# Causal mask of attention scores: added by VectorE in PSUM instead of by a third TensorE product, with two PSUM copies moved from VectorE to ScalarE

## The chip, the cores and the metric

One core of a Trainium2 chip runs the whole program. The metric is the device time of one execution in microseconds (us). The engines of the core are TensorE (PE in the rows, with its weight loads as PEld), VectorE (DVE), ScalarE (ACT), GpSimd (POOL) and SyncE (SP), which here only issues DMAs.

## The reference

The program computes a layer of causal attention plus a quantised linear layer, and after it a second layer of another kind. The change lies in the causal attention. Per batch entry (8 of them, 512 rows, 16 heads of 64):

```python
scores = jnp.einsum('bnqd,bnkd->bnqk', q, k) / jnp.sqrt(jnp.float32(L))
causal = jnp.arange(s)[None, :] <= jnp.arange(s)[:, None]
scores = jnp.where(causal, scores, -1000000000.0)
attn = jax.nn.softmax(scores, axis=-1)
attended = jnp.einsum('bnqk,bnkd->bnqd', attn, v)
```

## The kernel before, in words

The program has three stages: loading and scaling (about the first 140 us), a long software pipeline of "rings" that does the attention and the quantised layer, and the second layer. A ring `n` belongs to one pair of heads; there are 8 pairs in each of 8 batch entries, so 64 rings that matter, and a few to fill. With `b, r = n // 8, n % 8`, every engine walks through its own written-out order of steps, `ring(n)`, and the engines meet at semaphores. Nothing is reordered: an instruction that waits holds back all that stand behind it on its engine.

In ring `n` these things happen together:

- The scores of the next pair, `n + 1`, for head `h` = 0 and then 1. A head has four row blocks (tiles 0 to 3) of 128, 256, 384 and 512 columns, since the columns above the diagonal block are left out. Tile 3 lies in PSUM bank `sx`, tiles 0 and 2 together in `sy`, tile 1 in `sz`. TensorE makes each with two f16 products (L1328, L1329) and a third (L1330) that adds the mask to the diagonal block, as the product of an identity and a bf16 mask.
- VectorE takes the row maxima (`maxima`, L1021), ScalarE the exponentials with their row sums (`exps`, L698), VectorE the reciprocals of the sums (`inverse`, L1029), GpSimd scales the rows (`normalise`, L529).
- The rows of pair `n` are transposed by TensorE (`pt(n, j, h)`, L1341, column block `j`, 4 - `j` transposes) into one bank for head 0 (`pt0`) and one for head 1 (`pt1`). Each bank is copied out (`pt_whole(n, j)`): head 0 by ScalarE (L706), head 1 by VectorE (L1036). `pt(n, j, h)` waits for the copy of `j - 1`, as each head has but one bank. `av(n)` (L1355) then multiplies with the values; ScalarE's L714 follows it, once in each ring.
- The queries and keys of a later pair: `evens(n + 5)` and `odds(n + 5)` on TensorE, `even_terms` (L1000, L1001) and `odd_terms` (L1011, L1012) on VectorE, `rotate` (L501, L503) on GpSimd, `high_e` (L673) and `high_o` (L681) on ScalarE, then DMAs to and from a scratch. Rings 59 to 63 have none of this.
- From the second batch entry on, the output projection of the entry before (`attended`, L1370): 6 products after the scores (0,2) of head 0 and 6 after the scores (1) of head 1; in rings with `r % 4 == 0` the first of these is `ffn` (4 products) and the second has 12.

The orders of TensorE and ScalarE in a ring decide most of what follows. TensorE: `scores(n+1,0,(1))`, `v(n)`, `pt(n,0,0)`, `scores(n+1,0,(0,2))`, attended or ffn, `pt(n,0,1)`, `scores(n+1,0,(3,))`, `pt(n,1,0)`, `pt(n,1,1)`, `evens`, `scores(n+1,1,(1,))`, attended, `pt(n,2,0)`, `pt(n,2,1)`, `scores(n+1,1,(0,2))`, `pt(n,3,0)`, `scores(n+1,1,(3,))`, `pt(n,3,1)`, `odds`, `av(n)`. GpSimd: `normalise(n,1)`, `rotate`, two low parts, `normalise(n+1,0)`.

Of the kernel before, what the change touches and what calls it, by code (L numbers as in the profile page):

```python
# [10 lines left out]
P = 128  # L11
NT = SQ // P
# [9 lines left out]
MASKED = -1e30  # L22
OFF = [P * i * (i + 1) // 2 for i in range(NT + 1)]
TOFF = [sum(P * (NT - a) for a in range(j)) for j in range(NT + 1)]
# [19 lines left out]
def build(nc, x_d, weights_d, w8_d, bqk_d, vec_d, thr_d, gate_d, tab_d, out_d):  # L44
    f32, f16, bf16 = mybir.dt.float32, mybir.dt.float16, mybir.dt.bfloat16
    i8, i32, u32 = mybir.dt.int8, mybir.dt.int32, mybir.dt.uint32
    ALU = mybir.AluOpType
    ACT = mybir.ActivationFunctionType
# [7 lines left out]
    with ctx:  # L56
        def sb(name, shape, dt):
            return ctx.enter_context(nc.sbuf_tensor(name, shape, dt))

        def sem(name):  # L60
            return ctx.enter_context(nc.semaphore(name))
# [5 lines left out]
        wl = sb("wl", [P, C_END], f16)  # L67
        w8 = sb("w8", [P, KT, D], bf16)
        ident = sb("ident", [P, P], f32)
        identb = sb("identb", [P, P], bf16)  # L70
        maskb = sb("maskb", [P, P], bf16)

        bcol = sb("bcol", [P, NQ, 2, 2], f32)
        cosq = sb("cosq", [P, SQ], f32)
# [64 lines left out]
        kz = [carve(4 * SQ, f16).rearrange("p (h s) -> p h s", h=4) for _ in range(2)]  # L139
        vf = carve(NT * P).rearrange("p (t c) -> p t c", t=NT)  # L140
        pr = [carve(OFF[NT]) for _ in range(4)]
        ptf = [carve(TOFF[NT]) for _ in range(2)]
# [48 lines left out]
        consts = sem("consts")  # L191
# [39 lines left out]
        v_mm = sem("v_mm")  # L231
        vf_done = sem("vf_done")
        s_done = sem("s_done")
        max_done = sem("max_done")
        exp_done = sem("exp_done")
        rc_done = sem("rc_done")
        norm_done = sem("norm_done")
        pt_done = [sem(f"pt_done{h}") for h in range(2)]
        ptf_done = [sem(f"ptf_done{h}") for h in range(2)]
# [52 lines left out]
        def no_phase(f):  # L292

            return not 0 <= f < NPH

        def absent(n):

            return not 0 <= n < NR

        def after(engine, s, count):  # L300

            if not isinstance(count, int) or count > 0:
                engine.wait_ge(s, count)
# [41 lines left out]
        pj, wo, sx, sy, sz, pt0, pt1, ob = banks  # L345

        S_ORDER = [1, 0, 2, 3]
        s_tile = {3: sx[:, 0:512], 0: sy[:, 0:128], 2: sy[:, 128:512], 1: sz[:, 0:256]}

        S_BANK = {1: 1, 0: 2, 2: 2, 3: 3}  # L350
# [112 lines left out]
        def _(pool):  # L463

            pool.memset(ident[:], 0.0).then_inc(consts, 1)
            pool.memset(identb[:], 0.0).then_inc(consts, 1)
            pool.memset(maskb[:], 0.0).then_inc(consts, 1)
            pool.wait_ge(consts, 3)
            for m in (ident, identb):
                pool.affine_select(out=m[:], in_=m[:], compare_op=ALU.not_equal, fill=1.0, base=0,  # L470
                                   pattern=[[-1, P]], channel_multiplier=1).then_inc(consts, 1)
            pool.affine_select(out=maskb[:], in_=maskb[:], compare_op=ALU.is_ge, fill=MASKED, base=0,
                               pattern=[[-1, P]], channel_multiplier=1).then_inc(consts, 1)

            pool.wait_ge(wmax_done, NG)
# [2 lines left out]
            for g in range(NG):  # L478
                pool.wait_ge(whi_done, g + 1)
                if g in (G_Q, G_K):  # L480
                    for src, (high, low) in halves(g):
                        last = pool.tensor_tensor(low, src, high, ALU.subtract)
# [146 lines left out]
        @block.scalar  # L629
        def _(act):  # L630

            act.wait_ge(consts, 6)
            act.activation(nm3[:, 0, 0:1], ident[:, 0:1], ACT.Exp)
            def xt_high(batches):

# [26 lines left out]
            for t in range(2):  # L662
                act.activation(fbow[:, t], banks[7][:, 0:D], ACT.Copy)
                last = act.activation(wsxw[:, t], banks[7][:, D:2 * D], ACT.Copy)
# [10 lines left out]
            def high_o(f):  # L675

                if no_phase(f):
                    return
                act.wait_ge(r1_done, f + 1)
                after(act, hio_sent, 16 * f)  # L680
                act.activation(hi_o, r_o, ACT.Copy).then_inc(hio_done, 1)  # L681
# [8 lines left out]
            def exps(n, h, par, tiles):  # L690

                if absent(n):
                    return
                slot = 2 * par + h
                for i in tiles:

                    act.wait_ge(max_done, 4 * (2 * n + h) + {1: 1, 0: 3, 2: 3, 3: 4}[i])
                    act.activation(pr[slot][:, OFF[i]:OFF[i + 1]], s_tile[i], ACT.Exp, bias=nm[:, slot, i:i + 1],  # L698
                                   accum_out=sm[:, slot, i:i + 1]).then_inc(exp_done, 1)

            def pt_whole(n, j):

                if absent(n):
                    return
                act.wait_ge(pt_done[0], 4 * n + j + 1)
                act.activation(ptf[0][:, TOFF[j]:TOFF[j + 1]], pt0[:, 0:P * (NT - j)], ACT.Copy).then_inc(ptf_done[0], 1)  # L706

            def out_high(n):

# [6 lines left out]
            def ring(n):  # L716

                e, o = (n + 1) % 2, n % 2
                out_high(n - 1)
                exps(n + 1, 0, e, (1,))  # L720
                v_whole(n)
                pt_whole(n, 0)
                high_e(n + AHEAD - 1)
                exps(n + 1, 0, e, (0, 2))
                high_o(n + AHEAD - 1)
                pt_whole(n, 1)
                exps(n + 1, 0, e, (3,))
                pt_whole(n, 2)
                exps(n + 1, 1, e, (1, 0, 2))
                pt_whole(n, 3)  # L730
                exps(n + 1, 1, e, (3,))
# [130 lines left out]
        def _(dve):  # L862
# [97 lines left out]
            for g, by, dsts in ((G_Q, L ** -0.5, (cosq, sinq)), (G_K, 1.0, (cosk, sink))):  # L960
                for a, dst in enumerate(dsts):
                    dve.tensor_scalar(dst[:], tabraw[:, a], sc[:, g:g + 1], by, ALU.mult, ALU.mult)
                last = dve.tensor_scalar(bcol[:, :, g - G_Q], bcol[:, :, g - G_Q], inv[:, g:g + 1], None, ALU.mult)
# [4 lines left out]
            for k in range(KT):  # L968
                dve.tensor_scalar(diag[:, k], ident[:], fbo[:, k:k + 1], None, ALU.mult)
                last = dve.tensor_scalar(diag[:, KT + k], ident[:], vec[:, V_FS + k:V_FS + k + 1], None, ALU.mult)  # L970
# [43 lines left out]
            def maxima(n, h, par, tiles):  # L1014

                if absent(n):
                    return
                slot = 2 * par + h
                for i in tiles:
                    dve.wait_ge(s_done, 3 * (2 * n + h) + S_BANK[i])  # L1020
                    dve.tensor_reduce(nm[:, slot, i:i + 1], s_tile[i], AX.X, ALU.max, negate=True).then_inc(max_done, 1)  # L1021

            def inverse(n, h, par):
# [7 lines left out]
            def pt_whole(n, j):  # L1031

                if absent(n):
                    return
                dve.wait_ge(pt_done[1], 4 * n + j + 1)
                dve.tensor_copy(ptf[1][:, TOFF[j]:TOFF[j + 1]], pt1[:, 0:P * (NT - j)]).then_inc(ptf_done[1], 1)  # L1036
# [38 lines left out]
            def row_statistics(b):  # L1075

                dve.wait_ge(x1_done, 2 * b + 2)
                statistics(b * NT, b + NB)

            def ring(n):  # L1080

                b, r, e = n // NP, n % NP, (n + 1) % 2
                tail = b >= 1
                maxima(n + 1, 0, e, (1,))
                out_low(n - 1)
                maxima(n + 1, 0, e, (0, 2))
                pt_whole(n, 0)
                if tail and r % 4 == 0:
                    ffn_part(b - 1, r // 4)
                maxima(n + 1, 0, e, (3,))  # L1090
                pt_whole(n, 1)
                even_terms(n + AHEAD)
                inverse(n + 1, 0, e)
                maxima(n + 1, 1, e, (1,))
                pt_whole(n, 2)
                maxima(n + 1, 1, e, (0, 2, 3))
                pt_whole(n, 3)
                odd_terms(n + AHEAD)
                inverse(n + 1, 1, e)
                if n >= 0 and r >= NP - 4:  # L1100
                    quantise(b, r - NP + 4)
                if tail and r % 4 == 3:
                    residual(b - 1, r // 4)
                if b >= 2 and r == 1:
                    row_statistics(b - 2)
# [145 lines left out]

        @block.tensor
        def _(pe):
            pe.wait_ge(consts, 6)
            for b in range(NB):
                u = b % 2
                pe.wait_ge(xn1_done, b + 1)
# [1 line left out]
                for k in range(KT):  # L1259
                    for c in range(NT):  # L1260
                        last = pe.transpose(banks[2 * u + k][:, c * P:(c + 1) * P], xn1[u][:, c, k * P:(k + 1) * P], ident[:])
# [54 lines left out]
            def scores(n, h, tiles):  # L1316

                if absent(n):
                    return
                g = 2 * n + h  # L1320
                par, hh = n // 2 % 2, n % 2 * 2 + h
                if h == 0 and tiles[0] == 1 and hh == 0:
                    pe.wait_ge(q_in[par], 64 * (n // 4 + 1))
                    pe.wait_ge(k_in[par], 96 * (n // 4 + 1))
                after(pe, exp_done, 4 * g - 4 + {1: 1, 0: 3, 3: 4}[tiles[0]])
                for i in tiles:
                    out, q = s_tile[i], qs[par][:, hh, i * P:(i + 1) * P]
                    pe.matmul(out, q, kd[par][:, hh, 0:(i + 1) * P], start=True, stop=False)  # L1328
                    pe.matmul(out, q, kz[par][:, hh, 0:(i + 1) * P], start=False, stop=False)  # L1329
                    last = pe.matmul(out[:, i * P:(i + 1) * P], identb[:], maskb[:], start=False, stop=True)  # L1330
                last.then_inc(s_done, 1)

            def pt(n, j, h, par):
# [81 lines left out]
            for a in range(2 * KT):  # L1415
                last = pe.matmul(banks[7][:, a * P:(a + 1) * P], ones, diag[:, a], start=True, stop=True)
# [202 lines left out]
```

## Time and profile before

| | |
|---|---|
| median of 3 runs | 1176.16 us (1173.99 to 1178.44) |
| profiled execution, its own time | 1175.19 us |
| its span, first to last instruction | 1173.40 us |
| granted TensorE clock, mean share of full speed | 0.982 |
| TensorE products busy | 1023.0 us, 87% of the span |
| VectorE busy | 892.0 us, 76% |
| GpSimd busy | 767.5 us, 65% |
| ScalarE busy | 691.4 us, 59% |

The profile is one execution. A busy time counts an instruction from its start to its end, and neighbours on one engine overlap: a 128-column product is recorded with 0.22 us but the next one starts 0.06 us later. So what a product costs is read from the starts, not from its duration. An idle time stands in brackets with the instruction that ended it.

### The profile page before, as it was taken

To read this page: it belongs to the slowest core of one execution; us is meant where nothing else is said; L and a number is where in the kernel's file an instruction comes from. 1 tells how busy PE (TensorE), PEld (TensorE's weight loads), DVE (VectorE), ACT (ScalarE), POOL (GpSimd) and SP (SyncE) were. 2 spreads that over 40 slices of the span, in tenths; PEclk is the share of its full clock that TensorE was granted. 3 is DMA by queue.
4 is the path that set the end of the run, shared out by engine and by line. 5 is a ranking of instruction groups with operands and counts; after the bars stand their busy time and mean duration, and the time that the engine had idled before them with its cause. 6 is when DMAs were issued, how large, how long until landed. Compare 5 with 4: busy or idle time off the path is not lost.

```text
span 1173.4 us, 23304 instructions
## 1 busy us (share of the span) xinstructions
PE 1023.0 (87%) x7944; PEld 665.5 (57%) x7944; DVE 892.0 (76%) x1869; ACT 691.4 (59%) x1831; POOL 767.5 (65%) x949
## 2 busy tenths in 40 slices
PE   2004599999999999999999999999999965899988
PEld 1002266666666766766666676676667742454444
DVE  7695577776777777777777777777777637999996
ACT  1252366766666666666666666666667604766764
POOL 0081677777877777786777777687776515756762
PEclk9998999999999999999999999999999986999999
DMA  9203433342233233223323322322332000010001
GB/s 347 83 0 126 144 102 97 96 131 82 87 112 100 82 105 121 82 95 109 95 87 110 112 85 96 109 91 89 105 97 82 1 1 1 1 37 19 19 28 45
DMA packets 99700, 100.11 MB, mean 85 GB/s; under 512 B 12928, under 2 KB 94848, under 8 KB 99200
## 3 DMA queue, kind: packets, MB, share of 16 engines
q1 hardware_dynamic: 99584, 98.63, 25.8%
q8 instruction: 65, 1.06, 0.4%
q14 instruction: 51, 0.42, 0.1%
HBM read 56.64 MB, written 41.94 MB: 84 GB/s over the span
## 4 chain that ended last, share of the span: by engine, by line
PE 73%; DVE 18%; issue 3%; DMA 2%; ACT 2%; SPq 1%; POOL 1%; DVEq 0%; ACTq 0%; POOLq 0%
PE bank L1267 24%; PE bank L1355 13%; PE bank L1341 12%; PE bank L1370 7%; PE bank L1328 6%; PE bank L1329 5%; DVE arena L1179 3%; PE bank L1330 2%; DMA x_sb<-in_x 2%; PE bank L1517 2%; DVE nm L1149 1%; DVE arena L916 1%; DVE wmax L950 1%; DVE arena L1198 1%; DVE nm L1021 1%
## 5 line engine op out<-in xcount | busy, mean ns | idle before, releaser
L529 POOL TENSOR_SCALAR arena<-arena,rc 128x128 f32<-128x128 f32 (+3 forms) x512 | 276.0, 559 | 197.2 <-DVE rc L1029 197.2
L698 ACT ACTIVATE arena<-bank,nm 128x256 f32<-128x256 f32 (+3 forms) x512 | 268.4, 527 | 83.9 <-DVE nm L1021 73.7
L1021 DVE TENSOR_REDUCE nm<-bank 128x1 f32<-128x256 f32 (+3 forms) x512 | 229.9, 480 | 108.5 <-PE bank L1330 105.0
L1341 PE MATMUL bank<-ident,arena 128*128 128x128 f32 x1280 | 216.6, 277 | 4.8 <-DVE arena L1036 4.4
L1341 PEld LDWEIGHTS bank<-ident,arena 128*128 128x128 f32 x1280 | 143.7, 141 | 41.2 <-DVE arena L1036 20.3
L706 ACT ACTIVATE arena<-bank 128x512 f32<-128x512 f32 (+3 forms) x256 | 111.3, 435 | 79.6 <-PE bank L1341 79.4
L1329 PE MATMUL bank<-arena 128*128 128x256 f16 (+3 forms) x512 | 153.4, 300 | 0.0
L1355 PE MATMUL bank<-arena 128*64 128x512 f32 (+3 forms) x1024 | 152.0, 439 | 0.0
L1328 PE MATMUL bank<-arena 128*128 128x256 f16 (+3 forms) x512 | 147.4, 301 | 2.7 <-ACT arena L698 2.7
L1036 DVE COPY arena<-bank 128x512 f32<-128x512 f32 (+3 forms) x256 | 124.1, 485 | 23.8 <-PE bank L1341 20.0
L1355 PEld LDWEIGHTS bank<-arena 128*64 128x64 f32 x1024 | 67.8, 136 | 94.3 <-issue 71.3
L1267 PE MATMUL bank<-xsh,wh 128*128 128x512 f16 x256 | 98.1, 383 | 17.7 <-DVE arena L1001 9.6
L1330 PE MATMUL bank<-maskb,identb 128*128 128x128 bf16 x512 | 112.2, 219 | 0.0
L1370 PE MATMUL bank<-wh,arena 128*128 128x256 f16 x512 | 103.2, 278 | 7.2 <-DVE arena L1065 7.2
L698 ACT ACTIVATION_READ_ACCUMULATOR arena<-bank,nm 128x1 f32 x512 | 102.6, 200 | 0.0
L714 ACT ACTIVATE arena<-bank,bvs 128x512 f16<-128x512 f32 x64 | 44.0, 687 | 96.4 <-PE bank L1355 96.4
L1267 PE MATMUL bank<-xsl,wh 128*128 128x512 f16 x256 | 98.0, 383 | 0.0
L1267 PE MATMUL bank<-xsh,wl 128*128 128x512 f16 x256 | 98.0, 383 | 0.0
L501 POOL TENSOR_TENSOR arena<-arena 128x512 f32<-128x512 f32 x64 | 81.4, 1273 | 18.6 <-DVE arena L1012 18.6
L1267 PE MATMUL bank<-wh,xsh 128*128 128x128 f16 x512 | 89.1, 219 | 1.1 <-DVE arena L1012 1.1
L1267 PE MATMUL bank<-wh,xsl 128*128 128x128 f16 x512 | 89.1, 219 | 0.0
L1267 PE MATMUL bank<-wl,xsh 128*128 128x128 f16 x512 | 89.1, 219 | 0.0
(148 smaller groups left out, 2225.7 us busy)
## 6 DMA issues: line engine op xcount, KB each, us to landing
arena<-scr SPq DMA_DIRECT2D x320, 128.0 KB, 2.5
scr<-arena SPq DMA_DIRECT2D x256, 128.0 KB, 1.7
x_sb<-in_x SPq DMA_DIRECT2D x8, 512.0 KB, 6.5
arena<-in_weights SPq DMA_DIRECT2D x2, 2048.0 KB, 12.4
out<-x_sb SPq DMA_DIRECT2D x16, 256.0 KB, 2.2
xscr<-xsh SPq DMA_DIRECT2D x8, 256.0 KB, 2.3
xscr<-xsl SPq DMA_DIRECT2D x8, 256.0 KB, 2.2
xsh<-xscr SPq DMA_DIRECT2D x8, 256.0 KB, 3.1
```

What stands on the lines that cost most here:

```text
L529: last = pool.tensor_scalar(pr[slot][:, OFF[i]:OFF[i + 1]], pr[slot][:, OFF[i]:OFF[i + 1]], rc[:, slot, i:i + 1], 1.0, ALU.mult, ALU.mult)
L698: act.activation(pr[slot][:, OFF[i]:OFF[i + 1]], s_tile[i], ACT.Exp, bias=nm[:, slot, i:i + 1], accum_out=sm[:, slot, i:i + 1]).then_inc(e ...
L706: act.activation(ptf[0][:, TOFF[j]:TOFF[j + 1]], pt0[:, 0:P * (NT - j)], ACT.Copy).then_inc(ptf_done[0], 1)
L1021: dve.tensor_reduce(nm[:, slot, i:i + 1], s_tile[i], AX.X, ALU.max, negate=True).then_inc(max_done, 1)
L1036: dve.tensor_copy(ptf[1][:, TOFF[j]:TOFF[j + 1]], pt1[:, 0:P * (NT - j)]).then_inc(ptf_done[1], 1)
L1267: last = pe.matmul(out, lhs, rhs, start=(a == 0), stop=(a == len(pairs) - 1))
L1328: pe.matmul(out, q, kd[par][:, hh, 0:(i + 1) * P], start=True, stop=False)
L1329: pe.matmul(out, q, kz[par][:, hh, 0:(i + 1) * P], start=False, stop=False)
L1330: last = pe.matmul(out[:, i * P:(i + 1) * P], identb[:], maskb[:], start=False, stop=True)
L1341: last = pe.transpose(banks[5 + h][:, (i - j) * P:(i - j + 1) * P], pr[2 * par + h][:, OFF[i] + j * P:OFF[i] + (j + 1) * P], ident[:])
L1355: last = pe.matmul(ob[h * L:(h + 1) * L, j * P:SQ], vf[:, j, h * L:(h + 1) * L], ptf[h][:, TOFF[j]:TOFF[j + 1]], start=(j == 0), stop=(j = ...
L1370: last = pe.matmul(bank[:, t * D:(t + 1) * D], o[:, slot, rows], w[:, p, :], start=(p == 0 and a == 0 and t == 0), stop=(p == NP - 1 and a ...
```

## The change

TensorE's third product goes. VectorE adds an f32 mask to the diagonal block in PSUM before it takes the maxima: one add for tile 1, one for tiles 0 and 2 together (their diagonal blocks are columns 0 to 127 and 384 to 511 of `sy`), one for tile 3. After each add it waits for its own semaphore `masked`. Of head 1's four copies `j` = 0 and `j` = 2 go from VectorE to ScalarE. The score semaphore is counted per bank as before. On GpSimd the making of two bf16 constants is replaced by that of one f32 constant.

```diff
@@ scalar, ring
                 pt_whole(n, 0)
                 high_e(n + AHEAD - 1)
                 exps(n + 1, 0, e, (0, 2))
+                pt_whole(n, 0, 1)
                 high_o(n + AHEAD - 1)
                 pt_whole(n, 1)
                 exps(n + 1, 0, e, (3,))
                 pt_whole(n, 2)
+                pt_whole(n, 2, 1)
                 exps(n + 1, 1, e, (1, 0, 2))
                 pt_whole(n, 3)
@@ vector, maxima
                 slot = 2 * par + h
+                dve.wait_ge(s_done, 3 * (2 * n + h) + S_BANK[tiles[0]])
+                if tiles == (0, 2):
+                    both = sy[:].rearrange("p (a c) -> p a c", c=P)[:, 0:NT:NT - 1]
+                    dve.tensor_tensor(both, both, maskf[:].unsqueeze(1).broadcast_to([P, 2, P]), ALU.add).then_inc(masked, 1)
+                else:
+                    diagonal = s_tile[tiles[0]][:, tiles[0] * P:]
+                    dve.tensor_tensor(diagonal, diagonal, maskf[:], ALU.add).then_inc(masked, 1)
+                dve.wait_ge(masked, 3 * (2 * n + h) + S_BANK[tiles[0]])
                 for i in tiles:
-                    dve.wait_ge(s_done, 3 * (2 * n + h) + S_BANK[i])
                     dve.tensor_reduce(nm[:, slot, i:i + 1], s_tile[i], AX.X, ALU.max, negate=True).then_inc(max_done, 1)
@@ vector, ring
                 maxima(n + 1, 0, e, (0, 2))
-                pt_whole(n, 0)
                 if tail and r % 4 == 0:
                     ffn_part(b - 1, r // 4)
                 maxima(n + 1, 0, e, (3,))
@@
                 maxima(n + 1, 1, e, (1,))
-                pt_whole(n, 2)
-                maxima(n + 1, 1, e, (0, 2, 3))
+                maxima(n + 1, 1, e, (0, 2))
+                maxima(n + 1, 1, e, (3,))
                 pt_whole(n, 3)
@@ tensor, scores
                     pe.matmul(out, q, kd[par][:, hh, 0:(i + 1) * P], start=True, stop=False)
-                    pe.matmul(out, q, kz[par][:, hh, 0:(i + 1) * P], start=False, stop=False)
-                    last = pe.matmul(out[:, i * P:(i + 1) * P], identb[:], maskb[:], start=False, stop=True)
+                    last = pe.matmul(out, q, kz[par][:, hh, 0:(i + 1) * P], start=False, stop=True)
```

## Rows read from the trace of the kernel before

**Rows 1.** Busy time by stretch: us, busy (x count) per engine, PEclk, DMA share, GB/s

```profile
400.00:600.00 200.00, 200.00 (x1716) 137.00 (x1714) 152.28 (x332) 128.48 (x375) 151.01 (x198) 1.00 0.31 99
```

**Rows 2.** Timeline, ScalarE, the instruction after each `av`: start us, duration us

```profile
191.20 0.69 ACT L714 ACTIVATE arena<-bank,bvs 128x512 f16<-128x512 f32 x1 [1.48 <-PE bank L1355]
203.35 0.69 ACT L714 ACTIVATE arena<-bank,bvs 128x512 f16<-128x512 f32 x1 [1.48 <-PE bank L1355]
...
495.21 0.69 ACT L714 ACTIVATE arena<-bank,bvs 128x512 f16<-128x512 f32 x1 [1.55 <-PE bank L1355]
508.30 0.69 ACT L714 ACTIVATE arena<-bank,bvs 128x512 f16<-128x512 f32 x1 [1.68 <-PE bank L1355]
520.96 0.69 ACT L714 ACTIVATE arena<-bank,bvs 128x512 f16<-128x512 f32 x1 [1.55 <-PE bank L1355]
```

**Rows 3.** Chain that ended last, one ring: start us, us, what

```profile
523.57 0.06 PE bank L1330
...
525.21 0.84 PE bank L1341 x6
526.05 1.29 PE bank L1267 x6
```

**Rows 4.** Timeline, TensorE's products and weight loads at `pt(n,1,1)`

```profile
195.31 0.55 PE L1341 MATMUL bank<-ident,arena 128*128 128x128 f32 x3 [0.18 <-DVE arena L1036]
525.50 0.31 PEld L1341 LDWEIGHTS bank<-ident,arena 128*128 128x128 f32 x3 [0.20 <-DVE arena L1036]
```

**Rows 5.** Timeline, VectorE, one ring

```profile
523.67 0.76 DVE L1021 TENSOR_REDUCE nm<-bank 128x1 f32<-128x128 f32 x2 [1.23 <-PE bank L1330]
524.76 0.69 DVE L1036 COPY arena<-bank 128x512 f32<-128x512 f32 x1 [0.34 <-PE bank L1341]
...
527.38 0.75 DVE L1000 SCALAR_TENSOR_TENSOR arena<-bank,bcol,cosk 128x512 f32<-128x512 f32 x1 [0.74 <-PE bank L1267]
...
528.79 0.40 DVE L1021 TENSOR_REDUCE nm<-bank 128x1 f32<-128x256 f32 x1
529.11 0.41 DVE L1036 COPY arena<-bank 128x256 f32<-128x256 f32 x1
529.44 1.34 DVE L1021 TENSOR_REDUCE nm<-bank 128x1 f32<-128x128 f32 x3
...
532.64 0.17 DVE L1029 RECIPROCAL rc<-sm 128x4 f32<-128x4 f32 x1
```

**Rows 6.** Timeline, ScalarE, the same ring

```profile
523.98 0.63 ACT L673 ACTIVATE arena<-arena 128x512 f16<-128x512 f32 x1 [0.22 <-POOL arena L501]
524.51 0.35 ACT L698 ACTIVATE arena<-bank,nm 128x128 f32<-128x128 f32 x1
...
525.41 0.62 ACT L681 ACTIVATE arena<-arena 128x512 f16<-128x512 f32 x1
```

**Rows 7.** Timeline, GpSimd, four scalings of a head and a `rotate`

```profile
533.00 2.31 POOL L529 TENSOR_SCALAR arena<-arena,rc 128x128 f32<-128x128 f32 x4 [1.86 <-DVE rc L1029]
535.28 1.26 POOL L501 TENSOR_TENSOR arena<-arena 128x512 f32<-128x512 f32 x1
...
584.08 2.06 POOL L529 TENSOR_SCALAR arena<-arena,rc 128x128 f32<-128x128 f32 x4 [1.86 <-DVE rc L1029]
...
609.84 2.84 POOL L529 TENSOR_SCALAR arena<-arena,rc 128x128 f32<-128x128 f32 x4 [2.52 <-DVE rc L1029]
```

**Rows 8.** Groups, shapes apart: line, engine, tiles, count | busy us, mean ns | idle before

```profile
L706 ACT ACTIVATE arena<-bank 128x512 f32<-128x512 f32 x64 | 37.9, 592 | 0.0
L1036 DVE COPY arena<-bank 128x128 f32<-128x128 f32 x64 | 17.8, 279 | 0.4 <-PE bank L1341 0.4
L1065 DVE TENSOR_TENSOR arena<-bank,wsxw 128x512 f32<-128x512 f32 x16 | 10.9, 681 | 0.8 <-PE bank L1267 0.8
```

**Rows 9.** Timeline, VectorE, second layer, an instruction behind a wait on its own forerunner

```profile
1096.88 0.29 DVE L1153 TENSOR_SCALAR nb<-nm,sc_c,gate 128x2 f32<-128x2 f32 x1
1097.21 0.23 DVE L1155 TENSOR_SCALAR nb<-nb,gate 128x2 f32<-128x2 f32 x1
```

More of the change, by code:

```diff
@@ L69, in build @@
         ident = sb("ident", [P, P], f32)
-        identb = sb("identb", [P, P], bf16)
-        maskb = sb("maskb", [P, P], bf16)
+        maskf = sb("maskf", [P, P], f32)
         bcol = sb("bcol", [P, NQ, 2, 2], f32)
@@ L233, in build @@
         s_done = sem("s_done")
+        masked = sem("masked")
         max_done = sem("max_done")
@@ L465, in _ @@
             pool.memset(ident[:], 0.0).then_inc(consts, 1)
[L466 to L472, printed above, removed]
+            pool.memset(maskf[:], 0.0).then_inc(consts, 1)
+            pool.wait_ge(consts, 2)
+            pool.affine_select(out=ident[:], in_=ident[:], compare_op=ALU.not_equal, fill=1.0, base=0,
+                               pattern=[[-1, P]], channel_multiplier=1).then_inc(consts, 1)
+            pool.affine_select(out=maskf[:], in_=maskf[:], compare_op=ALU.is_ge, fill=MASKED, base=0,
                                pattern=[[-1, P]], channel_multiplier=1).then_inc(consts, 1)
@@ L630, in _ @@
         def _(act):
-            act.wait_ge(consts, 6)
+            act.wait_ge(consts, 4)
             act.activation(nm3[:, 0, 0:1], ident[:, 0:1], ACT.Exp)
@@ L699, in exps, with pt_whole @@
                                    accum_out=sm[:, slot, i:i + 1]).then_inc(exp_done, 1)
-            def pt_whole(n, j):
+            def pt_whole(n, j, h=0):
                 if absent(n):
                     return
-                act.wait_ge(pt_done[0], 4 * n + j + 1)
-                act.activation(ptf[0][:, TOFF[j]:TOFF[j + 1]], pt0[:, 0:P * (NT - j)], ACT.Copy).then_inc(ptf_done[0], 1)
+                act.wait_ge(pt_done[h], 4 * n + j + 1)
+                act.activation(ptf[h][:, TOFF[j]:TOFF[j + 1]], (pt0, pt1)[h][:, 0:P * (NT - j)], ACT.Copy).then_inc(ptf_done[h], 1)
             def out_high(n):
@@ L1253, in _ @@
         def _(pe):
-            pe.wait_ge(consts, 6)
+            pe.wait_ge(consts, 4)
             for b in range(NB):
```

## The prediction

> **What bounds the kernel now.** First the busy times by stretch. In the middle of the attention stage TensorE's products are busy for all of 200 us at full clock, VectorE and GpSimd for about three quarters, ScalarE for two thirds [rows 1]. So TensorE sets the pace and the other three have room, as an average. Second, the length of a ring, from one L714 to the next: 12.15 us in the first batch entry, 13.09 us in a ring with `r % 4 == 0` and 12.66 us in the others [rows 2]. There are 64 such rows: 8 rings of the first kind, 13 of the second, 38 of the third, and the last five. From ring 8 to 58 the mean is (2 x 13.09 + 6 x 12.66) / 8 = 12.77 us. Third, the chain that ended last, for what stands where in a ring, and the timelines for what TensorE waits for. It hardly waits, but the one place where it does is the place to watch: at `pt(n,1,1)` the weight load sat 0.20 us for VectorE's copy of `pt(n,0,1)` [rows 4], which ended at 524.76 + 0.69 = 525.45 [rows 5]. In the first batch entry, with less work on TensorE, the same wait holds the products themselves for 0.18 us [rows 4]. That is why those rings are not shorter by all the work that they lack. So the copy of `pt(n,0,1)` has no slack, and the change moves that very copy.
>
> **What the change takes away.** Eight L1330 products a ring. Each holds TensorE for 0.06 us (0.055 by 128-column neighbours) [rows 3], so 0.44 us a ring and 512 x 0.055 = 28 us in all. On VectorE two copies go: 0.69 us for 512 columns and 0.41 for 256 [rows 5].
>
> **What it adds.** Six adds a ring on VectorE, f32, one operand and the result in PSUM. The trace has no VectorE instruction that writes PSUM. The nearest is L1065, an add from PSUM and SBUF to SBUF, 0.681 us for 512 columns; a copy goes from 0.69 to 0.279 us between 512 and 128 columns [rows 5, 8], 1.07 ns a column. So 0.28 us for a 128-column add and 0.41 for the double one. Lower bound: nothing below this, since each add streams its columns; upper bound: twice as much, as GpSimd's add takes 1.26 us for 512 columns [rows 7]. I take the lower, as it is the same engine and the same operands but for the side of the result. Behind each add stands a wait for itself. Where VectorE waits for its own forerunner, the next starts 0.04 us after its end (1096.88 + 0.29 to 1097.21) [rows 9]; without a wait neighbours overlap by 0.08 (528.79 + 0.40 against 529.11) [rows 5]. So an add and its wait cost 0.32 us (128) or 0.45 (both), 2.18 us a ring, against 1.10 - 0.16 = 0.94 taken away. VectorE's busy share rises to about 85%, still not full; what matters is where the adds stand.
>
> A rule of the Trainium skill, "VectorE: DVE Perf Modes", section "The DRAIN you can't avoid", would have the waits free: a semaphore after each of eight copies cost nothing extra. The rows above disagree by 0.12 us for each; by the rule every add would be 0.12 us cheaper. This is taken up as a rival. The same page's section on the TRN2 errata gives (N + 151) / 0.96 ns for such an add, 0.29 and 0.42 us, which the trace's 0.681 us at 512 columns bears out.
>
> ScalarE gains a copy of 512 columns, 0.59 us [rows 8], and one of 256, some 0.38. The second stands just ahead of exps that wait for maxima anyway. The first is the one that counts. GpSimd's shorter making of constants lies in the first stage, ahead of the transposes that wait for normalised rows: nothing. The DMA issues do not move.
>
> **The moved copy inside one ring.** On ScalarE the copy of `pt(n,0,1)` now stands behind exps (0,2), and these behind the new add. Before, the maxima (0,2) start at 523.67. Three products less in front of them: 523.50. The double add and its wait: 523.95. The two maxima, 0.76: 524.71 [rows 5]. Exponentials from 524.75; ScalarE's next slot comes 525.41 - 524.51 = 0.90 later [rows 6], at 525.65. The copy, 0.59: 526.24, and TensorE goes on at 526.28, where it now does at 525.50. TensorE itself would be there at about 525.2 (from 523.57 to the three transposes before it), so it stands for a microsecond. The ring is 0.78 us longer to this point, and the four L1330 behind it give 0.22 back: 12.66 + 0.78 - 0.22 = 13.22 us.
>
> **The same copy from ring to ring.** ScalarE's order has a second way into exps (0,2): `high_e`, which waits for `rotate`, which stands on GpSimd behind `normalise(n,1)`. Already now `high_e` waits 0.22 us for it and ends only when the exps start [rows 6]. Now TensorE's go at `pt(n,1,1)` hangs on this chain, and the chain hangs on that go of the ring before: a closed loop. Its pieces: copy's end to even_terms 527.38 - 525.45 = 1.93; these two and the reciprocal 1.41; add and maximum of head 1's tile 1, 0.32 + 0.32 (0.40 less the overlap); adds of (0,2) and (3), 0.45 + 0.32, with three maxima 1.34 - 0.08 = 1.26; copy of `pt(n,3,1)` 0.20; odd_terms 1.33; reciprocal to scaling 533.00 - 532.64 = 0.36 [rows 5, 7]; four scalings 535.28 - 533.00 = 2.28; L501 and its semaphore 1.31 [rows 7]; `high_e` 0.53; exps 0.90 [rows 6]; copy 0.59; to TensorE 0.04. Sum 13.55 us. The scalings take 2.06 us in the rings in which VectorE does not quantise beside them, and 2.84 in one of eight [rows 7]: loops of 13.30 (r 0 to 3), 14.08 (r = 4) and 13.55 (r 5 to 7).
>
> Rings with `r % 4 == 0` have 0.66 us more of `attended` behind the go: 13.22 + 0.65 = 13.87 by TensorE for r = 0. In r = 4 about half of it, 0.33, reaches the loop, since TensorE is 0.3 us ahead of VectorE at the scores (0,2) of head 1: 14.41. Mean of eight: (13.87 + 3 x 13.30 + 14.41 + 3 x 13.55) / 8 = 13.60, 0.83 more than 12.77. Over 51 rings +42 us. In the first batch entry the loop is the same without `attended`, mean 13.49 against 12.15: 8 x 1.34 = +11. The last five rings have no loop, but three adds of head 1 or head 0 lie between TensorE and ScalarE: about 1 us each, +5. Six rings (r = 1, from the third entry on) carry row statistics on VectorE ahead of the next adds; I put about 0.9 us on each, a guess without a row, +5. Sum +63 or 64 us, with the 28 us of products already inside. The profiled execution's own time is 1175.2, 1.0 under the median; against the median the forecast is 1176.2 + 64 = 1240 us.
>
> **Rivals.** *Short loop.* The waits are nearly free, or the adds finish sooner than I take them, so that the loop shrinks under the way inside one ring. With 0.12 us off for each add: in-ring 13.22 - 0.12 = 13.10, the loop 13.55 - 0.36 = 13.19; mean about 13.33, so 51 x 0.56 + 8 x 1.0 + 9 = +46: 1222 us. This is also what the skill's rule on the wait would give. If only the in-ring way holds (GpSimd's chain has more slack than I read), 13.22 in ordinary rings: +28 + 5 + 5, 1214 us. Against both: the 0.04 us gap is in the rows, and `high_e` already ends exactly where the exps start. *Dear adds.* A write to PSUM takes up to twice the time: 0.97 us more in the loop, about 59 rings, 57 us: near 1297. For it: nothing in the trace shows such a write; against it: the same operands otherwise. *Faster, the other side.* The copy stays hidden and TensorE remains the pace: 28 us less products and 0.18 to 0.2 us less stall a ring in some, 1176 - 28 = 1148 us, or 1140 at best. It decides at one point: ScalarE's copy has to end before TensorE is at `pt(n,1,1)`, at 525.2 less the three products; by the rows it ends at 526.24, and even without any add ScalarE's slot at 525.41 and 0.59 give 526.00. For it speaks only that TensorE is at 100% and the others not. *No change*: a gain of 28 us and an equal loss, 0.44 us of stall a ring; my sum has more than twice that.
>
> **Chances and range.** The loop as summed 0.50, short loop or in-ring way alone 0.26, dear adds (over 1272) 0.12, faster 0.09, within half a per cent 0.03. Half a per cent, 6 us, is about what a measurement of this kernel can tell from no change. The range for 8 in 10 goes from 1204, a little under the in-ring case, to 1272, where half of the dear adds' price would be paid. Slower then has 0.88.
>
> **What would show it.** In the profile after, L714 to L714 should be 13.2 to 13.6 us in ordinary rings and no longer 12.16 us in the first entry but the same as later. TensorE should be idle for about a microsecond a ring ahead of L1341, released by ScalarE's copy, with its busy share in the middle of the stage near 92 to 94%, and the clock still full. `high_e` should stand directly behind L501 and in front of exps (0,2). The add should show 0.28 and 0.41 us, the maximum 0.04 us behind it. The prediction is wrong if TensorE has no idle time at L1341, if its idle time is released by VectorE's maxima or by `v`'s wait for odd_terms, or if the adds take more than 0.35 us for 128 columns.

## The result, and the profile after

The changed kernel takes 1246.57 us (median of 4 runs, 1245.06 to 1247.56); the kernel before, with one more run, 1175.53 us. The ratio is 1.060, 95% interval 1.0575 to 1.0625. It is slower, 6.6 us above the forecast of 1240 and inside the range. The profiled execution took 1245.06 us, 69.9 more than that of before, with a span of 1243.3 us.

Busy time by stretch of the changed kernel, columns as in [rows 1]:

```profile
400.00:600.00 200.00, 181.56 (x1487) 121.80 (x1486) 155.92 (x364) 130.35 (x380) 139.48 (x183) 1.00 0.29 93
```

TensorE was busy for 200 of these 200 us; now it is for 91% at the same clock. No other engine took its place: VectorE went up by 4 us only, and GpSimd fell. This kernel is slower although every engine has room, so it is held by waits: a chain of steps on several engines, each released by the one before.

The instruction after each `av` (it is L712 now), which marks the rings, as [rows 2]:

```profile
171.30 0.69 ACT L712 ACTIVATE arena<-bank,bvs 128x512 f16<-128x512 f32 x1 [0.23 <-PE bank L1360]
184.59 0.69 ACT L712 ACTIVATE arena<-bank,bvs 128x512 f16<-128x512 f32 x1 [0.23 <-PE bank L1360]
...
514.99 0.69 ACT L712 ACTIVATE arena<-bank,bvs 128x512 f16<-128x512 f32 x1 [0.88 <-PE bank L1360]
528.27 0.69 ACT L712 ACTIVATE arena<-bank,bvs 128x512 f16<-128x512 f32 x1 [0.88 <-PE bank L1360]
...
569.57 0.69 ACT L712 ACTIVATE arena<-bank,bvs 128x512 f16<-128x512 f32 x1 [0.88 <-PE bank L1360]
583.10 0.69 ACT L712 ACTIVATE arena<-bank,bvs 128x512 f16<-128x512 f32 x1 [0.88 <-PE bank L1360]
```

The first two rings of the first batch entry have 13.29 us each, for 12.15 (its others 13.08 to 14.96). Of the later ordinary rings, one without VectorE's quantising beside it has 13.28, and one with it 13.53 to 13.76, for 12.66. So the rings of the first entry, which have less TensorE work, are no longer shorter than the others. That is the mark of a loop that TensorE's work is not in.

TensorE and ScalarE at the place that was forecast (timeline; compare [rows 4, 6]):

```profile
561.64 0.55 PE L1346 MATMUL bank<-ident,arena 128*128 128x128 f32 x3 [1.32 <-ACT arena L704]
575.17 0.55 PE L1346 MATMUL bank<-ident,arena 128*128 128x128 f32 x3 [1.26 <-ACT arena L704]
```

```profile
573.10 0.63 ACT L671 ACTIVATE arena<-arena 128x512 f16<-128x512 f32 x1 [0.79 <-POOL arena L499]
573.63 0.35 ACT L696 ACTIVATE arena<-bank,nm 128x128 f32<-128x128 f32 x1
...
574.53 0.59 ACT L704 ACTIVATE arena<-bank 128x512 f32<-128x512 f32 x1
```

TensorE stands at `pt(n,1,1)` until ScalarE's copy is done, for 1.3 us in these two rings and 1.0 to 1.5 us in the ordinary ones from the third batch entry on. The exps in front of the copy follow `high_e` (L671) without a gap, and `high_e` waits 0.79 us for GpSimd. The rest of the loop, VectorE and GpSimd, from the go at 561.64 to the next one:

```profile
563.52 0.75 DVE L1000 SCALAR_TENSOR_TENSOR arena<-bank,bcol,cosk 128x512 f32<-128x512 f32 x1 [0.74 <-PE bank L1273]
...
564.93 0.27 DVE L1025 TENSOR_TENSOR bank<-bank,maskf 128x128 f32<-128x128 f32 x1
565.24 0.42 DVE L1028 TENSOR_REDUCE nm<-bank 128x1 f32<-128x256 f32 x1
565.58 0.42 DVE L1022 TENSOR_TENSOR bank<-bank,maskf 128x256 f32<-128x256 f32 x1
566.04 0.76 DVE L1028 TENSOR_REDUCE nm<-bank 128x1 f32<-128x128 f32 x2
566.71 0.29 DVE L1025 TENSOR_TENSOR bank<-bank,maskf 128x128 f32<-128x128 f32 x1
567.04 0.69 DVE L1028 TENSOR_REDUCE nm<-bank 128x1 f32<-128x512 f32 x1
567.64 0.28 DVE L1043 COPY arena<-bank 128x128 f32<-128x128 f32 x1
567.84 0.74 DVE L1011 SCALAR_TENSOR_TENSOR arena<-bank,bcol,sink 128x512 f32<-128x512 f32 x1
...
569.16 0.17 DVE L1036 RECIPROCAL rc<-sm 128x4 f32<-128x4 f32 x1
```

```profile
569.53 2.30 POOL L527 TENSOR_SCALAR arena<-arena,rc 128x128 f32<-128x128 f32 x4 [2.25 <-DVE rc L1036]
571.79 1.27 POOL L499 TENSOR_TENSOR arena<-arena 128x512 f32<-128x512 f32 x1
```

VectorE has no gap from 563.52 to the reciprocal, and each add's reader starts 0.04 us after the add's end. From go (the start of `pt(n,1,1)`) to go it is 575.17 - 561.64 = 13.53 us; the sum of the prediction was 13.55.

The groups of the adds, as [rows 8]:

```profile
L1025 DVE TENSOR_TENSOR bank<-bank,maskf 128x128 f32<-128x128 f32 x256 | 74.0, 289 | 23.0 <-PE bank L1335 22.5
...
L1022 DVE TENSOR_TENSOR bank<-bank,maskf 128x256 f32<-128x256 f32 x128 | 54.9, 429 | 45.2 <-PE bank L1335 45.1
```

### The profile page after: what moved, and what is told of

The parts are those of the page before. It is cut to its first block, busy times and chain, and to the rows that moved or that the text cites. A ratio compares the mean times of both kernels' runs of the same rounds, so it can differ in the third digit from the quotient of the medians.

```text
span 1243.3 us, 22661 instructions
## 1 busy us (share of the span) xinstructions
PE 1006.9 (81%) x7432; PEld 639.4 (51%) x7432; DVE 953.1 (77%) x2125; ACT 734.9 (59%) x1959; POOL 766.6 (62%) x947
## 4 chain that ended last, share of the span: by engine, by line
DVE 37%; PE 26%; POOL 12%; ACT 11%; issue 10%; DMA 2%; SPq 1%; DVEq 0%; POOLq 0%; ACTq 0%
PE bank L1273 12%; POOL arena L527 7%; DVE nm L1028 6%; ACT arena L696 5%; POOL arena L499 5%; PE bank L1346 4%; PE bank L1375 3%; DVE arena L1011 3%; ACT arena L704 3%; DVE arena L1000 3%; DVE arena L1185 3%; DVE arena L1001 3%; DVE arena L1012 2%; PE bank L1360 2%; DVE bank L1022 2%
## 5 line engine op out<-in xcount | busy, mean ns | idle before, releaser
L1346 PE MATMUL bank<-ident,arena 128*128 128x128 f32 x1280 | 220.5, 279 | 89.2 <-ACT arena L704 87.4
L1028 DVE TENSOR_REDUCE nm<-bank 128x1 f32<-128x256 f32 (+3 forms) x512 | 239.6, 489 | 13.2
L704 ACT ACTIVATE arena<-bank 128x512 f32<-128x512 f32 (+3 forms) x384 | 167.2, 454 | 99.4 <-PE bank L1346 99.3
L1346 PEld LDWEIGHTS bank<-ident,arena 128*128 128x128 f32 x1280 | 148.5, 141 | 144.0 <-ACT arena L704 118.8
L1335 PE MATMUL bank<-arena 128*128 128x256 f16 (+3 forms) x512 | 154.7, 303 | 0.0
L1334 PE MATMUL bank<-arena 128*128 128x256 f16 (+3 forms) x512 | 141.5, 303 | 2.2 <-ACT arena L696 2.2
L1043 DVE COPY arena<-bank 128x384 f32<-128x384 f32 (+1 forms) x128 | 53.6, 419 | 74.2 <-PE bank L1346 74.2
L1025 DVE TENSOR_TENSOR bank<-bank,maskf 128x128 f32<-128x128 f32 x256 | 74.0, 289 | 23.0 <-PE bank L1335 22.5
L1022 DVE TENSOR_TENSOR bank<-bank,maskf 128x256 f32<-128x256 f32 x128 | 54.9, 429 | 45.2 <-PE bank L1335 45.1
L517 POOL TENSOR_TENSOR arena<-arena 128x512 f16<-128x512 f32 x64 | 74.1, 1158 | 24.7 <-ACT arena L679 24.7
```

The costliest lines, as they stand in the source:

```text
L704: act.activation(ptf[h][:, TOFF[j]:TOFF[j + 1]], (pt0, pt1)[h][:, 0:P * (NT - j)], ACT.Copy).then_inc(ptf_done[h], 1)
L1022: dve.tensor_tensor(both, both, maskf[:].unsqueeze(1).broadcast_to([P, 2, P]), ALU.add).then_inc(masked, 1)
L1335: last = pe.matmul(out, q, kz[par][:, hh, 0:(i + 1) * P], start=False, stop=True)
L1346: last = pe.transpose(banks[5 + h][:, (i - j) * P:(i - j + 1) * P], pr[2 * par + h][:, OFF[i] + j * P:OFF[i] + (j + 1) * P], ident[:])
```

## The experiments

Eleven kernels ran. Ratios are to the kernel before, in runs on the same chip.

**1. The copy of `pt(n,0,1)` back on VectorE**, all else as changed:

```diff
@@ scalar, ring
                 exps(n + 1, 0, e, (0, 2))
-                pt_whole(n, 0, 1)
@@ vector, ring
                 maxima(n + 1, 0, e, (0, 2))
+                pt_whole(n, 0)
```

> The changed kernel with the copy of pt(n,0,1) back on VectorE, where it stood before; the adds on VectorE and the copy of pt(n,2,1) on ScalarE stay. Theory (the moved copy of column block 0 closes the loop, the adds alone are hidden): TensorE is the pace again, no idle time at the transposes of pt(n,1,1), rings of about 12.1 to 12.2 us, total 1143 to 1155 us, less than the kernel before. Rival (VectorE's adds alone make it the pace, the copy only moves load): a ring of 13.2 us or more, total 1210 to 1245 us.

1167.88 us, ratio 0.994 (0.992 to 0.996): all of the loss gone, and a little gain. The theory holds for the direction and the rival falls. The number was missed: rings of 12.33 us, not 12.1 to 12.2. So the adds are not wholly hidden. TensorE still waits at the same transposes, now for VectorE's copy, which stands behind the double add. In an ordinary ring only the weight load waits, as in the kernel before; in a ring with `ffn` the products do too (VectorE and TensorE, timeline):

```profile
597.95 0.68 DVE L1042 COPY arena<-bank 128x512 f32<-128x512 f32 x1
```

```profile
586.35 0.31 PEld L1346 LDWEIGHTS bank<-ident,arena 128*128 128x128 f32 x3 [0.30 <-DVE arena L1042]
...
598.68 0.55 PE L1346 MATMUL bank<-ident,arena 128*128 128x128 f32 x3 [0.28 <-DVE arena L1042]
```

The weight load waits 0.30 us where it waited 0.20 [rows 4]. So of the 0.44 us of products a ring about 0.1 is paid back, and 12.66 becomes 12.33.

**2. Both copies back on VectorE**, only the adds: as experiment 1 and

```diff
@@ scalar, ring
-                pt_whole(n, 2, 1)
@@ vector, ring
                 maxima(n + 1, 1, e, (1,))
+                pt_whole(n, 2)
```

> The changed kernel with both of head 1's copies back on VectorE: only the adds in place of the third product. Theory: the copy of pt(n,2,1) now ends behind an add and a maximum (0.32 us later), and pt(n,3,1) waits about 0.3 us for it; rings of about 12.4 to 12.5 us, total 1155 to 1165 us. Rival (VectorE as the pace): 1210 us or more.

1190.81 us, ratio 1.014 (1.012 to 1.016), rings of 12.80 us. The place was right and the price too low, by 26 us against the top of the expected range: beside the wait at `pt(n,1,1)`, `pt(n,3,1)` waits for the copy that stands behind an add and a maximum. That makes the ring 0.47 us longer than in experiment 1, where about 0.3 us had been expected (weight load and product):

```profile
577.78 0.14 PEld L1346 LDWEIGHTS bank<-ident,arena 128*128 128x128 f32 x1 [0.73 <-DVE arena L1041]
...
577.79 0.33 PE L1346 MATMUL bank<-ident,arena 128*128 128x128 f32 x1 [0.24 <-DVE arena L1041]
```

**3. Only the two copies moved**, third product kept, no adds: the kernel before with `pt_whole(n, 0, 1)` and `pt_whole(n, 2, 1)` in ScalarE's ring and without them in VectorE's.

> The kernel before with only the two copies moved to ScalarE, third product kept, no adds. Theory: without the adds the loop is only 12.5 us long, so the way inside one ring holds: the copy ends 0.5 us later than VectorE's, rings of 13.1 to 13.2 us, total about 1200 to 1210 us, with TensorE idle at pt(n,1,1) behind ScalarE's copy. Rival (only the adds cost): 1176 us or less, as VectorE is relieved.

1217.10 us, ratio 1.036 (1.033 to 1.038). Without a single add the copies alone cost 42 us. Rings of 13.17 us were as expected; the total was 7 us over the top of the range. Rings with `r % 4 == 0` take 13.83 us and those with `r` = 5 13.68, which I had left out. In the profiled execution some 4 us more lie ahead of the pipeline: VectorE's scaling of `wsxw`, which precedes the first maxima, starts at 136.69 us for 132.60, in a stage whose code is the one of before. Among the five kernels that keep the third product this start lies anywhere from 131.63 to 136.69 us, so it need not be a price of the copies. TensorE waits for ScalarE:

```profile
561.04 0.55 PE L1341 MATMUL bank<-ident,arena 128*128 128x128 f32 x3 [0.47 <-ACT arena L706]
574.21 0.55 PE L1341 MATMUL bank<-ident,arena 128*128 128x128 f32 x3 [0.69 <-ACT arena L706]
```

Copies alone +42, adds alone +16, both +71: 13 us come only together. Some 5 of them are falls of TensorE's clock in the trace of the changed kernel (last section), which the rings of the other two traces do not show. The others fit adds that lengthen a loop which the copy closed, but no run separates them.

**4. `high_e` behind the copy**, which takes GpSimd out of the loop:

```diff
@@ scalar, ring
                 pt_whole(n, 0)
-                high_e(n + AHEAD - 1)
                 exps(n + 1, 0, e, (0, 2))
                 pt_whole(n, 0, 1)
+                high_e(n + AHEAD - 1)
```

> The changed kernel with ScalarE's high_e behind the exps (0,2) and the copy of pt(n,0,1) instead of ahead of them: GpSimd is taken out of the loop, all else stays. Theory (GpSimd's chain holds the exps): the copy goes by the maxima, rings of about 13.2 us in all kinds but r % 4 == 0, and VectorE's idle time in the maxima grows; total 1210 to 1225 us. Rival (the way inside one ring is the pace and GpSimd only seems to be): no change, 1246 us.

1228.10 us, ratio 1.046 (1.044 to 1.048), 18 us less than the changed kernel: every ordinary ring now 13.27 or 13.28 us, quantising beside it or not, and 12.91 in the first entry. So GpSimd's chain did hold the exps in half of the rings (`r` = 5, 6, 7 and 0) and in the first entry. In `r` = 1 to 3 the way inside one ring is as long, 13.27 for 13.28, so there the two cannot be told apart. The total was 3 us over the expectation. What stays is the way inside one ring (ScalarE and TensorE):

```profile
577.17 0.37 ACT L696 ACTIVATE arena<-bank,nm 128x128 f32<-128x128 f32 x1 [0.56 <-DVE nm L1028]
...
578.08 0.59 ACT L704 ACTIVATE arena<-bank 128x512 f32<-128x512 f32 x1
```

```profile
578.73 0.55 PE L1346 MATMUL bank<-ident,arena 128*128 128x128 f32 x3 [1.22 <-ACT arena L704]
```

Its exps wait for VectorE's maxima, where before they followed `high_e`.

**5 and 6. One more add, of zeros, with its wait**, in head 1's tile 3 or in head 0's tiles (0,2). Adding zeros leaves the scores as they are. (`zerof` is made once, on GpSimd; that line is left out below.)

```diff
@@ vector, maxima, experiment 5
                 dve.wait_ge(masked, 3 * (2 * n + h) + S_BANK[tiles[0]])
+                if h == 1 and tiles == (3,):
+                    dve.tensor_tensor(s_tile[3][:, 3 * P:], s_tile[3][:, 3 * P:], zerof[:], ALU.add).then_inc(again, 1)
+                    dve.wait_ge(again, n + 1)
@@ vector, maxima, experiment 6
+                if h == 0 and tiles == (0, 2):
+                    dve.tensor_tensor(s_tile[0], s_tile[0], zerof[:], ALU.add).then_inc(again, 1)
+                    dve.wait_ge(again, n + 1)
```

> The changed kernel with one more add of 128 columns (of zeros, to the same diagonal block) and its wait for head 1's tile 3: 0.32 us more of VectorE in a part that the loop from ring to ring goes through. Theory (that loop is the pace): every ring with projections 0.32 us longer, 13.28 becomes 13.60, total +18 to +20 us over the changed kernel, about 1265 us. Rival (the way inside one ring is the pace): no change.

> The changed kernel with one more add of 128 columns (of zeros, to tile 0) and its wait for head 0's tiles 0 and 2: 0.32 us more in the way inside one ring, outside the loop through GpSimd. Theory: in rings with r = 5 to 7, where exps (0,2) wait for GpSimd and not for the maxima, most of it is hidden (0 to 0.1 us); in rings r = 0 to 3, where the two ways are within 0.1 us of each other, 0.2 to 0.3 us; total +6 to +12 us over the changed kernel. Rival (VectorE's own load is the pace): +0.32 us a ring as for head 1, +20 us.

Head 1: 1263.79 us (ratio 1.074, 1.070 to 1.078), 17 us over the changed kernel. Head 0: 1256.64 us (1.069, 1.067 to 1.071), 10 us over it. The same work on the same engine, at two places, has two prices. A ring that quantises, head 1 first and then head 0:

```profile
583.44 0.69 ACT L715 ACTIVATE arena<-bank,bvs 128x512 f16<-128x512 f32 x1 [0.69 <-PE bank L1366]
597.31 0.69 ACT L715 ACTIVATE arena<-bank,bvs 128x512 f16<-128x512 f32 x1 [0.69 <-PE bank L1366]
```

```profile
576.16 0.69 ACT L715 ACTIVATE arena<-bank,bvs 128x512 f16<-128x512 f32 x1 [0.88 <-PE bank L1366]
589.77 0.69 ACT L715 ACTIVATE arena<-bank,bvs 128x512 f16<-128x512 f32 x1 [0.88 <-PE bank L1366]
```

13.87 and 13.61 us, for 13.53: head 1's add is paid whole, head 0's in 0.08 us, as there the exps wait for GpSimd. In rings without quantising head 0's add gives 13.61 for 13.28, and head 1's 13.62 in `r` = 2 and 3 but only 13.32 in `r` = 1, where the expectation had the whole price. The intervals of the two ratios touch (1.070 to 1.078, 1.067 to 1.071), and it is the rings that tell the two apart. VectorE's load is not the pace; the place of the add is.

**7, 8, 9. `evens` ahead of `pt(n,1,1)`**, so that the late copy has 1.29 us of other work in front of its reader:

```diff
@@ tensor, ring
                 pt(n, 1, 0, o)
-                pt(n, 1, 1, o)
                 evens(n + AHEAD)
+                pt(n, 1, 1, o)
```

On top of experiment 1:

> As add_copy0_dve (copy of pt(n,0,1) on VectorE), and TensorE does evens ahead of pt(n,1,1) instead of behind it, so that the copy has 1.29 us more. Theory (what is left of the wait at pt(n,1,1) costs TensorE its last tenths): the idle time there goes, rings of 12.05 to 12.2 us, total 1143 to 1158 us. Rival (VectorE is by now the pace, since even_terms start later by the copy of pt(n,1,1)): a new wait of TensorE for odd_terms or even_terms, 12.33 us or more, total 1165 us or more.

1152.58 us, ratio 0.981 (0.979 to 0.983), rings of 12.05 and 12.14 us: faster than both kernels.

```profile
400.00:600.00 200.00, 198.38 (x1643) 134.67 (x1641) 178.90 (x422) 136.51 (x404) 156.21 (x204) 1.00 0.32 101
```

TensorE is busy throughout again, and VectorE for 89%, 23 us more than in the slow kernel's same stretch. So VectorE's load as such does not slow this kernel.

On top of experiment 4:

> As high_e_late (both copies on ScalarE, high_e behind them), and evens ahead of pt(n,1,1). Theory (the copy is 1.1 us late by ScalarE's order, and 1.29 us of other work in front of its reader hides it): the wait at pt(n,1,1) goes and the ring falls from 13.27 to 12.1 to 12.4 us, total 1150 to 1170 us. Rival (VectorE or ScalarE is the pace in itself): the ring stays over 13 us and the wait moves elsewhere, total 1210 us or more.

1167.56 us, ratio 0.994 (0.992 to 0.996), rings of 12.22 us. With both copies on ScalarE and all adds, the mere order of steps, one moved on TensorE and one on ScalarE, takes 79 us off the changed kernel.

On the kernel before, alone:

> The kernel before with nothing but evens ahead of pt(n,1,1): it says what this order alone is worth without adds and without moved copies. Theory: the 0.18 us at pt(n,1,1) go, rings of 12.48 us for 12.66, total 1163 to 1168 us. Rival: the wait moves to a later copy, 1175 us.

1183.04 us, ratio 1.005 (1.004 to 1.007): the theory fell. The rival named the right kind of place, a later copy, but had no loss there (1175 us). The rings are 12.87 us. VectorE's copy of `pt(n,1,1)` now comes after `evens` and pushes even_terms back, and with them the copy of `pt(n,2,1)`, for which `pt(n,3,1)` waits (VectorE, TensorE):

```profile
531.66 0.56 DVE L1036 COPY arena<-bank 128x384 f32<-128x384 f32 x1 [1.16 <-PE bank L1341]
532.14 0.74 DVE L1000 SCALAR_TENSOR_TENSOR arena<-bank,bcol,cosk 128x512 f32<-128x512 f32 x1
...
533.85 0.41 DVE L1036 COPY arena<-bank 128x256 f32<-128x256 f32 x1
```

```profile
534.32 0.33 PE L1341 MATMUL bank<-ident,arena 128*128 128x128 f32 x1 [0.18 <-DVE arena L1036]
```

**10 and 11. The third product kept, and only the copy of `pt(n,2,1)` on ScalarE**, in the order of before and with `evens` ahead. The edit is `pt_whole(n, 2, 1)` in ScalarE's ring as in the change, `pt_whole(n, 2)` out of VectorE's, and for 11 the order of experiment 7.

> The kernel before (third product kept, no adds) with only the copy of pt(n,2,1) moved to ScalarE. Beside add_copy0_dve it says what the adds in place of the product are worth. Theory (this copy was no cost in ordinary rings): rings of 12.6 to 12.66 us, only the first batch entry shorter by the 0.36 us that pt(n,3,1) waits there; total 1170 to 1175 us. Rival (ScalarE is late with it too): 1178 us or more.

> As product_copy2, and evens ahead of pt(n,1,1): the best order found, with the third product instead of the adds. Theory (before_evens_first lost because even_terms and then the copy of pt(n,2,1) on VectorE came late for pt(n,3,1); on ScalarE that copy is in time): rings of 12.44 to 12.50 us, total 1160 to 1167 us, so that the adds are worth 0.3 to 0.4 us a ring beside it. Rival (the loss was another's): 1180 us as before_evens_first.

1170.95 us (ratio 0.997, 0.996 to 0.998) and 1162.49 us (0.989, 0.988 to 0.991), both as expected, with 12.66 and 12.48 us for an ordinary ring. With that copy on ScalarE the order of `evens` gains where it lost before, so experiment 9's loss lay where it was read. Beside experiments 1 and 7 they also show what the adds gain in place of the third product, all else equal: 3 us (1170.95 to 1167.88) in the old order, 10 us (1162.49 to 1152.58) in the new one. In the old order most of the 0.33 us of an ordinary ring is lost elsewhere: rings of the first entry go from 11.58 to 11.96, rings with row statistics from 12.66 to 13.21.

## Why the prediction was right, point by point

**The bound and the place.** TensorE set the pace, and `pt(n,1,1)` was where it lost it. Shown by experiments 1 and 3: putting one copy back recovers the loss, moving the copies alone makes more than half of it.

**The loop.** Its sum, 13.55 us, was measured as 13.53, and 13.30 as 13.28; the adds were taken as 0.28 and 0.41 us and took 0.289 and 0.429. The 13.28 is no test of the loop by itself, as the way inside one ring is 13.27 (experiment 4). The loop is tested where the two differ: in the first entry, 13.29 against 12.91, in the rings with quantising beside them, and by the two added adds. By the Trainium skill, "VectorE: DVE Perf Modes", section on the TRN2 errata, an estimate for the adds is 0.29 and 0.42 us; the rows agree, although here the result goes to PSUM, of which its formula does not speak. An add's own wait costs 0.12 us, as the prediction took it: with a wait 564.93 + 0.27 = 565.20, next 565.24; without one 565.24 + 0.42 = 565.66, next 565.58. By the same page of the Trainium skill, section "The DRAIN you can't avoid", a semaphore after each of eight copies cost nothing extra; this trace does not agree.

**The sum.** Between L714 and L712 rows of the same ring: rings 0 to 8 grew by 12.4 us (forecast 11), rings 8 to 58 by 51.2 (forecast 42, and 5 for the row statistics), the last five by 3.2 (forecast 5), and 3.3 us came before ring 0, where I had put nothing. Together 70.1. The eight kinds of ring sum up to 108.9 us for a batch entry without statistics, against 108.8 forecast, but that is luck in part, as single rings are off both ways: `r` = 0 has 14.20 us (13.87 forecast), `r` = 4 13.95 (14.41), `r` = 5 13.76 (13.55). Two terms were misplaced. Each quantising step stands at the end of VectorE's ring, so it lengthens the scalings of the next ring, and the long one of 2.83 us counts to `r` = 5 (the last step to `r` = 0). And the 0.66 us of `attended` come whole on top of the loop in both `r` = 0 (13.53 + 0.66 = 14.19) and `r` = 4 (13.28 + 0.66 = 13.94). The statistics cost 14.30 - 13.28 = 1.0 us in each of six rings, for which I had guessed 0.9 without a row.

**What it missed.** The clock was to stay full; in the profiled execution it fell three times among the rings, about 5 us together (last section): 1.7 of the first entry's 12.4 us and 3.4 of the 51.2. Of the 3.3 us before ring 0, 2.3 are there before the first add: the scaling of `wsxw` starts at 134.86 us for 132.60, well inside the scatter named in experiment 3. The other 1.0 us is not explained by a run. The last five rings gave 1.8 us less than forecast. So the total came within 6.6 us partly because misses of both signs met. VectorE's share was forecast as about 85%, by the old length of a ring; in the longer ring it is 78%.

**The rivals.** *Short loop*: refuted, the wait is in the rows; but experiment 4 shows the in-ring way by itself, 13.27 us for the 13.22 worked out. Its total was 1228 us where the prediction put 1214 for that case; the sum there has no term for the first entry, where rings of 12.91 us for 12.15 cost 6 us. *Dear adds*: refuted by their durations. *Faster*: refuted for this change, and its condition was the right one. Experiments 7 and 8 meet it, by giving the copy something to hide behind, and experiment 7 ends at 1152.58 us, near the 1148 of that rival.

## What to carry to other kernels

Work taken off a full engine is worth its time only if no wait of that engine lengthens. Before moving a step to a less busy engine, find its reader and the moment at which the reader arrives, and what stands ahead of the step in the new engine's order. Here a copy of 0.59 us that had no slack was set behind two exponentials which themselves stood behind a chain through VectorE and GpSimd; 42 of the 71 us come from the moved copies without any add. And where a copy has to be late, give its reader other work first: the same exchanged pair of steps was worth 61 us (experiment 8 against 4) and 15 us (7 against 1) and cost 7 (experiment 9), depending on what stood behind it.

## What the runs showed of the hardware that was not expected

TensorE's granted clock fell among the rings of the changed kernel, which it never did between 200 and 800 us in the kernel before. Busy time by stretch of the changed kernel (PEclk is the third number from the end), and the ring around the second fall:

```profile
190.00:197.00 7.00, 6.40 (x29) 3.39 (x29) 3.53 (x9) 3.34 (x10) 3.33 (x5) 0.76 0.51 161
...
610.00:617.00 7.00, 5.19 (x58) 3.98 (x54) 5.95 (x19) 4.25 (x12) 5.66 (x7) 1.00 0.06 21
617.00:624.00 7.00, 7.00 (x35) 3.85 (x35) 4.35 (x11) 3.08 (x11) 3.21 (x5) 0.76 0.19 64
624.00:631.00 7.00, 6.89 (x66) 4.87 (x65) 4.94 (x13) 4.97 (x14) 4.80 (x7) 1.00 0.23 69
```

```profile
615.03 0.55 PE L1346 MATMUL bank<-ident,arena 128*128 128x128 f32 x3 [0.44 <-ACT arena L704]
616.94 0.55 PE L1346 MATMUL bank<-ident,arena 128*128 128x128 f32 x3 [1.37 <-ACT arena L704]
```

```profile
626.55 0.69 ACT L712 ACTIVATE arena<-bank,bvs 128x512 f16<-128x512 f32 x1 [1.19 <-PE bank L1360]
639.83 0.69 ACT L712 ACTIVATE arena<-bank,bvs 128x512 f16<-128x512 f32 x1 [0.88 <-PE bank L1360]
```

This is a ring with row statistics, in which TensorE stands 0.44 and 1.37 us within two microseconds; it was busy for 5.19 of 7 us before the fall. Part of the next stretch ran at 1.2 in place of 2.4 GHz, and the ring took 15.98 us where its like take 14.30, so 1.7 us for one fall. It came in two of the six such rings in this execution. The first fall, at about 191 us, came in the first entry behind a wait of 1.88 us; that ring took 14.96 us for the 13.29 of its neighbours, again 1.7 us (the next ring, 13.08, may give 0.2 back), although its neighbours have the same wait. And more idle time need not bring a fall. In the trace of experiment 8 TensorE once stood for 3.35 us and the clock stayed full:

```profile
664.00:671.00 7.00, 4.89 (x56) 3.84 (x52) 6.87 (x15) 1.31 (x4) 5.80 (x8) 1.00 0.23 72
671.00:678.00 7.00, 5.75 (x37) 3.56 (x38) 5.62 (x15) 5.90 (x18) 3.45 (x5) 1.00 0.21 72
```

```profile
672.25 0.55 PE L1346 MATMUL bank<-ident,arena 128*128 128x128 f32 x3 [3.35 <-ACT arena L704]
```

What decides which wait brings a fall is open.
